# A convolution-attention hybrid on one Trainium2 core: local attention issued in a new order, group norm folded into a product

## Chip, cores and metric

The program runs on one core of one Trainium2 chip. The metric is the device time of one execution in microseconds (us). The core has five instruction queues: TensorE (PE in the profile, with PEld for its weight loads), VectorE (DVE), ScalarE (ACT), GpSimd (POOL) and SyncE (SP), which issues most transfers. Each queue runs in order, and the queues wait for each other by semaphores.

## What is computed

The input is x of 16 images, 56x56 positions, 32 channels, float32. Cut to what matters here:

```python
x = x + local(_gn(x))           # _gn: 32 groups of 1 channel, over H and W, per image
t = x.reshape(16, 3136, 32)
t = t + attention(_ln(t))       # one head over 3136 tokens, plus its input
t = t + experts(_ln(t))         # 16 experts, each pooling its top 8 tokens

def local(x):                   # windows of 7x7, 4 heads of 8 channels, hidden width 128
    h = roll(_ln(x), (3, 3))    # cut into 64 windows of 49 tokens
    q, k, v = split(h @ qkv_w.T + qkv_b)
    a = softmax(q @ k.T / sqrt(8) + bias)
    o = _ln((a @ v) @ out_w.T + out_b)
    return gelu(o @ mlp_w1.T + mlp_b1) @ mlp_w2.T + mlp_b2
```

## The kernel before

The work has four stages. **Setup** loads x in 4 groups of 4 images, brings channels to partitions (4 images x 32 channels = 128) through PE transposes, stores the image with 3 wrapped rows above it in `ximg` (rows of 56), takes the group norm's mean and variance (`gn`) and prepares weights. **Local attention** follows, the stage that the change rewrites. **Global attention** (lines 1607 to 1669) and the **experts** are straight-line code and are not touched.

Local attention runs over 32 chunks (`G * NC`): a chunk is one row of 8 windows of 4 images, that is 392 columns (`CT`) on 128 partitions. A chunk has three parts.

- The part ahead ("pre"): `group_norm` on DVE subtracts the image's mean, scales and wraps 3 columns into `xg`; `center_window` (PE) takes the channel mean away by a product with a constant matrix; ACT squares it, PE averages the squares (`variance`), ACT takes log and exp (`root`), DVE multiplies (`normalize`, k=0); PE forms queries and keys (`project`), ACT and DVE copy them with masks (`queries`, `keys`).
- The main part, four units u of two windows each: `scores` (PE, 8 products), bias added and row maxima (DVE, lines 1047 and 1052), `subtract` (POOL, 544), `exponentials` (ACT, 699), `sums` with a reciprocal (DVE, 1058 and 1061), `probabilities` (POOL, 550), `transposes` (PE, 8 into two banks), `probs_a` (ACT, 703) copies the first bank and `probs_b` (DVE, 1065) the second, `values` (PE) and `values_copy` (DVE, 1072), `weighted_values` (PE, 16 products), `weighted_copy` (ACT, 711).
- The part behind ("post"): `out_projection`, a second norm (k=1), four `hidden` products with four `gelu`, `mlp_out`, `skip_connection` (DVE), `center_sum` and a third norm (k=2), `residual` (POOL), and two stores by SP.

All engines write the work out by hand in a function `chunk(it, ...)` of their own: the post part of chunk it-1, the main part of it and the pre part of it+1 are woven together. The scores, exponentials and probabilities are double buffered by u % 2; the PSUM banks XB, YB and ZB are shared by all the projections and norms. Chunks 0 and 1 (2 and 3 on some engines) and the last two are written out, the rest is a hardware loop (`Fori`) of two chunks an iteration, in which semaphore targets and image rows come from registers. `scores_first` waits for queries and keys and issues a one-column dummy product (line 1425) ahead of unit 0's scores. GELU needs another ACT table set than log and exp do, so a load stands at each change (shown as ACT_TABLE_LOAD, lines 695 and 725).

## Time and profile before

| | us |
|---|---|
| median of 3 runs | 3136.1 (3134.99 to 3137.02) |
| the profiled execution's own time | 3140.94 |
| its span in the profile | 3139.1 |
| setup, to the first `center_window` | 83.2 |
| local attention, first to last `out_projection` (line 1480) | 125.8 to 981.1 |
| experts and stores, from about | 3030 |

A row of the page or of a group of instructions gives the line, the engine, the operation, what it writes and reads with partitions x elements, how often, busy time and mean ns of one, and the idle time before it with what ended it. A row of a timeline gives start, duration and, in brackets, the wait ahead of it. fp32 products appear twice in the counts (x16 for 8 products), and the stated end of a product is modelled: the distance between the starts of two neighbouring groups tells what a group costs PE. PEclk is the clock granted to TensorE as a share of full speed.

### The profile page before, as it was taken

To read this page: it belongs to the slowest core of one execution; us is meant where nothing else is said; L and a number is where in the kernel's file an instruction comes from. 1 tells how busy PE (TensorE), PEld (TensorE's weight loads), DVE (VectorE), ACT (ScalarE), POOL (GpSimd) and SP (SyncE) were. 2 spreads that over 40 slices of the span, in tenths; PEclk is the share of its full clock that TensorE was granted. 3 is DMA by queue.
4 is the path that set the end of the run, shared out by engine and by line. 5 is a ranking of instruction groups with operands and counts; after the bars stand their busy time and mean duration, and the time that the engine had idled before them with its cause. 6 is when DMAs were issued, how large, how long until landed. Compare 5 with 4: busy or idle time off the path is not lost.

```text
span 3139.1 us, 61958 instructions
## 1 busy us (share of the span) xinstructions
PE 2864.7 (91%) x25025; PEld 1320.0 (42%) x25025; DVE 2416.2 (77%) x3155; ACT 2112.6 (67%) x3837; POOL 614.5 (20%) x493
## 2 busy tenths in 40 slices
PE   3788888888886899999999999999999999999987
PEld 3344444444442534344344344344344443443446
DVE  6788888888883787887887877787887877877844
ACT  2477767767764557777777777777777777777762
POOL 0344444444442010110100101101100101101100
PEclk6899999999997989999999999999999999999997
DMA  3000000000002811011011010010110110110003
GB/s 89 1 16 15 15 15 13 13 15 15 15 16 90 286 18 22 1 22 22 1 22 21 2 22 10 13 22 1 22 22 1 22 22 1 22 22 1 1 1 84
DMA packets 93851, 81.05 MB, mean 26 GB/s; under 512 B 62452, under 2 KB 83541, under 8 KB 92629
## 3 DMA queue, kind: packets, MB, share of 16 engines
q1 hardware_dynamic: 92085, 78.26, 9.5%
q8 instruction: 138, 2.26, 0.3%
q14 instruction: 60, 0.49, 0.0%
q10 hardware_dynamic: 1568, 0.04, 0.0%
HBM read 39.57 MB, written 32.11 MB: 23 GB/s over the span
## 4 chain that ended last, share of the span: by engine, by line
PE 68%; issue 11%; ACT 7%; POOL 6%; DVE 5%; DMA 2%; ACTq 1%; POOLq 0%; SPq 0%; DVEq 0%
PE ps L1635 19%; PE ps L1607 18%; PE ps L1659 17%; POOL arena L544 4%; PE ps L1669 3%; PE ps L1619 2%; POOL arena L550 2%; PE ps L1487 1%; ACT arena L699 1%; ACT L725 1%; ACT arena L817 1%; PE ps L1714 1%; DMA arena<-in_x 1%; POOL arena L560 1%; DVE arena L1052 1%
## 5 line engine op out<-in xcount | busy, mean ns | idle before, releaser
L1211 DVE TENSOR_REDUCE arena<-ps 128x2 f32<-128x896 f32 (+1 forms) x1408 | 1455.8, 1078 | 366.9 <-PE ps L1607 366.7
L837 ACT ACTIVATE arena<-ps 128x512 f32<-128x512 f32 (+1 forms) x2464 | 1270.7, 602 | 354.0 <-PE ps L1635 339.7
L1635 PE MATMUL ps<-arena 97*128 97x512 f16 (+1 forms) x2800 | 819.1, 357 | 9.4 <-ACT arena L837 1.2
L1607 PE MATMUL ps<-arena 96*128 96x448 f16 x2800 | 773.1, 358 | 10.8 <-DVE arena L1201 8.2
L1659 PE MATMUL ps<-arena 128*32 128x512 f32 (+2 forms) x7328 | 666.6, 456 | 0.7 <-DVE arena L1233 0.7
L1635 PEld LDWEIGHTS ps<-arena 97*128 97x128 f16 (+1 forms) x2800 | 252.0, 99 | 438.3 <-ACT arena L837 169.8
L1659 PEld LDWEIGHTS ps<-arena 128*32 128x32 f32 x7328 | 235.8, 109 | 408.7 <-ACT arena L837 193.1
L609 POOL TENSOR_TENSOR tok<-arena,tok 128x128 f32<-128x128 f32 (+1 forms) x112 | 47.4, 423 | 1556.4 <-DVE arena L1233 1556.4
L1607 PEld LDWEIGHTS ps<-arena 96*128 96x128 f16 x2800 | 225.2, 99 | 298.5 <-DVE arena L1211 114.4
L550 POOL TENSOR_TENSOR arena<-arena 113x784 f32<-113x784 f32 x128 | 192.4, 1503 | 431.2 <-DVE arena L1061 431.2
L544 POOL TENSOR_TENSOR arena<-arena 113x784 f32<-113x784 f32 x128 | 192.2, 1502 | 129.3 <-DVE arena L1052 129.3
L1058 DVE TENSOR_REDUCE arena<-arena 113x16 f32<-113x784 f32 x128 | 123.6, 965 | 59.9 <-ACT arena L699 59.9
L699 ACT ACTIVATE arena<-arena 113x784 f32<-113x784 f32 x128 | 109.4, 855 | 64.8 <-POOL arena L544 64.5
L1487 PE MATMUL ps<-arena,w1f 128*128 128x392 f32 x256 | 123.1, 565 | 26.0 <-ACT arena L725 23.9
L1458 PE MATMUL ps<-cst,arena 113*128 113x113 f32 x1024 | 127.2, 268 | 10.6 <-POOL arena L550 6.9
L824 ACT ACTIVATE arena<-ps 128x512 f32<-128x512 f32 x96 | 57.3, 597 | 107.9 <-PE ps L1659 107.9
L1052 DVE TENSOR_REDUCE arena<-arena 113x16 f32<-113x784 f32 x128 | 124.2, 970 | 4.5
L1458 PEld LDWEIGHTS ps<-cst,arena 113*128 113x128 f32 x1024 | 104.1, 142 | 41.3 <-POOL arena L550 25.1
L1047 DVE TENSOR_TENSOR arena<-ps,relb 113x784 f32<-113x784 f32 x128 | 116.9, 913 | 2.4 <-PE ps L1432 2.0
L817 ACT ACTIVATE arena<-ps 1x512 f16<-1x512 f32 (+1 forms) x112 | 60.0, 536 | 86.2 <-PE ps L1619 86.0
L1432 PE MATMUL ps<-arena 64*49 64x196 f32 x2048 | 117.1, 344 | 0.1
L1065 DVE COPY arena<-ps 128x452 f32<-128x452 f32 x128 | 79.5, 621 | 45.8 <-PE ps L1458 45.8
(181 smaller groups left out, 2787.6 us busy)
## 6 DMA issues: line engine op xcount, KB each, us to landing
arena<-qk_scratch SPq DMA_DIRECT2D x96, 196.0 KB, 4.0
qk_scratch<-arena SPq DMA_DIRECT2D x16, 448.0 KB, 4.8
arena<-ximg SPq DMA_DIRECT2D x16, 400.0 KB, 6.6
arena<-in_x SPq DMA_DIRECT2D x4, 1568.0 KB, 8.4
xa_scratch<-arena SPq DMA_DIRECT2D x32, 196.0 KB, 1.9
res_scratch<-arena SPq DMA_DIRECT2D x32, 196.0 KB, 2.1
arena<-xa_scratch SPq DMA_DIRECT2D x4, 1568.0 KB, 9.2
arena<-res_scratch SPq DMA_DIRECT2D x4, 1568.0 KB, 13.0
```

Source lines behind the costliest of these rows:

```text
L544: pool.tensor_tensor(s3, s3, mx[0:113, i, :].rearrange("p (m o) -> p m o", o=1) .broadcast_to([113, GB * NH, L]), ALU.subtract).then_inc(c ...
L550: pool.tensor_tensor(pr[0:113, i, :].rearrange("p (m k) -> p m k", k=64)[:, :, 0:L], ex[0:113, i, :].rearrange("p (m k) -> p m k", k=L), m ...
L699: act.activation(ex[0:113, u % 2, :], sc[0:113, u % 2, :], ACT.Exp).then_inc(conv["exp"], 1)
L837: act.activation(pk[0:rows, x % DEPTH, QC * m:QC * m + n], ps[0:rows, w % SB, 0:n], ACT.Exp, scale=float(C) ** -0.5).then_inc(att["exp"], 1)
L1052: dve.tensor_reduce(mx[0:113, i, :], sc[0:113, i, :].rearrange("p (m k) -> p m k", k=L), AX_X, ALU.max)\
L1058: dve.tensor_reduce(mx[0:113, 2 + i, :], ex[0:113, i, :].rearrange("p (m k) -> p m k", k=L), AX_X, ALU.add)\
L1211: dve.tensor_reduce(mxp[0:rows, p, 2 * u:2 * u + k], ps[0:rows, at_:at_ + k, 0:KN], AX_X, ALU.max)\
L1458: last = pe.transpose(ps[:, PT_ + k, 128 * n:128 * n + 113], pr[0:113, i, 128 * m:128 * m + 128], ident(113))
L1487: pe.matmul(ps[:, (XB, XB, XB, YB)[j], 0:CT], w1f[:, j, :], xn2[:, :], start=True, stop=True)\
L1607: last = pe.matmul(ps[0:rows, MB + 2 * (j % 2) + n % 2, 0:KN], q2[p][0:96, T * t:T * t + rows], k2[p][0:96, KN * m:KN * m + KN], start=Tru ...
L1635: last = pe.matmul(ps[0:rows, bank, at_ % QC:at_ % QC + chunk_cols(c)], k2[p][0:97, T * t:T * t + rows], q2[p][0:97, QC * c:QC * c + chunk ...
L1659: last = pe.matmul(ps[C * g:C * (g + 1), AVB, w * h:w * h + w], vf[p][:, t, :], pk[:, x % DEPTH, at_ + w * h:at_ + w * h + w], start=(t < ...
```

## The change

- Every engine's part of local attention is one Python loop over k, without `Fori`: all 32 chunks are straight-line code with constant semaphore targets. A step k works on four chunks: the last norms and the MLP of k, the units of k+1 and k+2, and the centring product of k+3. Waits are written only where the order needs them; the dummy product is gone.
- `group_norm` and `xg` are gone. The group norm's scale is multiplied into the centring matrix, one per image group (`cg`), and its mean into a bias of the product's result (`gnc`), which `square` and `normalize` (k=0) add. `center_window` reads the image itself. `ximg` therefore has rows of 59 (3 wrapped columns) and the product reads it in the order window, row, column, 7 elements at a stretch, where it read 392 in a row before; `normalize` (k=0), which did the reordering, now reads and writes plainly.
- In setup, the statistics are taken from PSUM (7 of 448 elements for 8 of 392), the copy into `ximg` writes rows of 59, and two copies fill the wrapped columns.
- Of the four copies of the second transposed bank in a chunk, those of units 1 and 3 go to ACT (`probs_b`, semaphore `pcopy_c`).

```diff
-        ximg = sb("ximg", [128, G * HALO, W])
+        ximg = sb("ximg", [128, G * HALO, WIDE])
         xf = ximg[:, :, :].rearrange("p r c -> p (r c)")[:, 0:B * NT * C].rearrange(
             "p (t b c) -> p t b c", b=B, t=NT)
...
+                if k == 0:
+                    act.activation(sq[:, :], ps[:, YB, 0:CT], ACT.Square, bias=gnc[:, n // NC:n // NC + 1])\
...
+            def probs_b(u):
+                act.activation(pt[:, u % 2, 4 * 113:8 * 113].rearrange("p (n q) -> p n q", q=113),
+                               ps[:, PT_ + 1, :].rearrange("p (n q) -> p n q", q=128)[:, :, 0:113], ACT.Copy)\
+                   .then_inc(conv["pcopy_c"], 1)
...
+            for k in range(-2, CHUNKS):
+                if on(k):
+                    act.wait_ge(ln[1]["var"], k + 1)
+                    log_of(1)
+                if on(k + 2):
+                    act.wait_ge(ln[0]["center"], k + 3)
+                    square(k + 2, 0)
+                if on(k + 1):
+                    probs_a(0)
+                if on(k):
+                    act.wait_ge(ln[1]["std"], k + 1)
+                    rstd(1)
+                if on(k + 2):
+                    act.wait_ge(ln[0]["var"], k + 3)
+                    log_of(0)
+                    act.wait_ge(ln[0]["std"], k + 3)
+                    rstd(0)
+                if on(k + 1):
+                    act.wait_ge(conv["ptrans"], 8 * k + 12)
+                    probs_a(1)
+                if on(k):
+                    act.wait_ge(conv["hid"], 4 * k + 1)
+                    gelu(0)
+                if on(k + 1):
+                    probs_b(1)
+                    act.wait_ge(conv["av"], 4 * k + 5)
+                    weighted_copy(0)
+                if on(k + 2):
+                    act.wait_ge(conv["qk"], 2 * k + 5)
+                    queries(k + 2)
+                if on(k):
+                    act.wait_ge(conv["hid"], 4 * k + 2)
+                    gelu(1)
+                if on(k + 1):
+                    act.wait_ge(conv["sub"], 4 * k + 8)
+                    exponentials(3)
+                    act.wait_ge(conv["ptrans"], 8 * k + 14)
+                    probs_a(2)
+                    act.wait_ge(conv["av"], 4 * k + 6)
+                    weighted_copy(1)
+                if on(k):
+                    act.wait_ge(conv["hid"], 4 * k + 3)
+                    gelu(2)
+                    act.wait_ge(conv["hid"], 4 * k + 4)
+                    gelu(3)
+                if on(k + 1):
+                    act.wait_ge(conv["av"], 4 * k + 7)
+                    weighted_copy(2)
+                log_and_exp()
+                if on(k + 1):
+                    act.wait_ge(conv["ptrans"], 8 * k + 16)
+                    probs_a(3)
+                if on(k + 2):
+                    act.wait_ge(conv["sub"], 4 * k + 9)
+                    exponentials(0)
+                if on(k + 1):
+                    probs_b(3)
+                if on(k):
+                    act.wait_ge(ln[2]["center"], k + 1)
+                    square(k, 2)
+                if on(k + 1):
+                    act.wait_ge(conv["av"], 4 * k + 8)
+                    weighted_copy(3)
+                if on(k):
+                    act.wait_ge(ln[2]["var"], k + 1)
+                    log_of(2)
+                    act.wait_ge(ln[2]["std"], k + 1)
+                    rstd(2)
+                if on(k + 1):
+                    act.wait_ge(ln[1]["center"], k + 2)
+                    square(k + 1, 1)
+                if on(k + 2):
+                    act.wait_ge(conv["sub"], 4 * k + 10)
+                    exponentials(1)
+                    act.wait_ge(conv["sub"], 4 * k + 11)
+                    exponentials(2)
...
-                img = ximg[:, g * HALO:(g + 1) * HALO, :].rearrange("p r c -> p (r c)")
+                img = image(g, 0, HALO)
                 for n in range(NK):
                     dve.wait_ge(s_xt, NK * g + n + 1)
-                    dve.tensor_copy(img[:, SHIFT * W:].rearrange("p (q j) -> p j q", j=SP)[:, 4 * n:4 * n + 4, :],
-                                    ps[:, n, 0:KN].rearrange("p (j q) -> p j q", j=4)).then_inc(s_xe, 1)
+                    dve.bn_stats(bns[:, n, :], ps[:, n, 0:KN])
+                    dve.tensor_copy(img[:, SHIFT:, SHIFT:].rearrange("p r (h j) -> p j r h", j=SP)[:, 4 * n:4 * n + 4],
+                                    ps[:, n, 0:KN].rearrange("p (j r h) -> p j r h", j=4, h=2)).then_inc(s_xe, 1)
                 dve.wait_ge(s_xe, NK * (g + 1))
-                dve.tensor_copy(img[:, 0:SHIFT * W], img[:, H * W:HALO * W])
-                for c in range(NC):
-                    last = dve.bn_stats(bns[:, c, :], img[:, SHIFT * W + CT * c:SHIFT * W + CT * (c + 1)])
-                step(last)
-                step(dve.bn_aggr(gn[:, g, 0:2], bns[:, :, :].rearrange("p c s -> p (c s)")))
+                dve.tensor_copy(img[:, 0:SHIFT, SHIFT:], img[:, H:HALO, SHIFT:])
+                dve.tensor_copy(img[:, 0:SHIFT, 0:SHIFT], img[:, H:HALO, W:WIDE])
+                step(dve.tensor_copy(img[:, SHIFT:, 0:SHIFT], img[:, SHIFT:, W:WIDE]))
+                step(dve.bn_aggr(gn[:, g, 0:2], bns[:, 0:NK, :].rearrange("p c s -> p (c s)")))
...
             step(dve.reciprocal(gn[:, :, 3], gn[:, :, 2]))
+            for g in range(G):
+                last = dve.tensor_scalar(cg[:, g, :], cv("center"), gn[:, g, 3:4], None, ALU.mult)
+            step(last)
...
+            dve.tensor_scalar(gnc[:, :], ps[:, 6, 0:G], -1.0, None, ALU.mult)
...
                 if k == 0:
-                    def rows(v):
-                        return v.rearrange("p (r w c) -> p r w c", r=WS, c=WS)
-                    last = dve.tensor_tensor(dst.rearrange("p (w r c) -> p r w c", r=WS, c=WS), rows(src),
-                                             rows(rs[:, k, :]), ALU.mult)
+                    dve.scalar_tensor_tensor(xn[:, n % 2, :], ps[:, YB, 0:CT], gnc[:, n // NC:n // NC + 1], rs[:, 0, :], ALU.add,
+                                             ALU.mult).then_inc(ln[0]["norm"], 1)
...
+                if on(k):
+                    dve.wait_ge(conv["y"], 2 * k + 2)
+                    if on(k - 1):
+                        dve.wait_ge(conv["rt"], k)
+                    skip_connection(k)
...
+            for g in range(G):
+                pe.matmul(ps[:, 6, g:g + 1], cg[:, g, :], gn[:, g, 0:1], start=True, stop=True)
             pe.matmul(ps[:, 4, 3:4], wp[:, 256:384], bv[:, BV:BV + 1], start=True, stop=False)
...
             def center_window(n):
-                pe.wait_ge(conv["xg"], n + 1)
-                pe.matmul(ps[:, YB, 0:CT], cv("center"), xg[:, :], start=True, stop=True).then_inc(ln[0]["center"], 1)
+                pe.matmul(ps[:, YB, 0:CT], cg[:, n // NC, :],
+                          image(n // NC, n % NC * WS, WS)[:, :, 0:W].rearrange("p r (w c) -> p w r c", c=WS),
+                          start=True, stop=True).then_inc(ln[0]["center"], 1)
...
+            for k in range(-3, CHUNKS):
+                if on(k + 2):
+                    pe.wait_ge(ln[0]["norm"], k + 3)
+                    project_queries(k + 2)
+                    project_keys(k + 2)
+                if on(k):
+                    pe.wait_ge(conv["gelu"], 4 * k + 1)
+                    hidden(1)
+                if on(k + 1):
+                    pe.wait_ge(conv["pcopy_c"], 2 * k + 3)
+                    pe.wait_ge(conv["prob"], 4 * k + 7)
+                    transposes(2)
+                    pe.wait_ge(conv["oc"], 4 * k + 5)
+                    values(k + 1, 2)
+                if on(k + 2):
+                    pe.wait_ge(conv["kz"], k + 3)
+                    pe.wait_ge(conv["qz"], k + 3)
+                    scores(0)
+                if on(k + 1):
+                    pe.wait_ge(conv["vcopy"], 4 * k + 7)
+                    weighted_values(1)
+                if on(k):
+                    pe.wait_ge(conv["gelu"], 4 * k + 2)
+                    hidden(2)
+                    hidden(3)
+                if on(k + 2):
+                    pe.wait_ge(conv["bias"], 4 * k + 9)
+                    scores(1)
+                if on(k + 1):
+                    pe.wait_ge(conv["pcopy_b"], 2 * k + 4)
+                    pe.wait_ge(conv["oc"], 4 * k + 6)
+                    weighted_values(2)
+                if on(k):
+                    mlp_out((0, 1))
+                    pe.wait_ge(conv["gelu"], 4 * k + 4)
+                    mlp_out((2, 3))
+                if on(k + 1):
+                    pe.wait_ge(conv["prob"], 4 * k + 8)
+                    transposes(3)
+                    pe.wait_ge(conv["oc"], 4 * k + 7)
+                    values(k + 1, 3)
+                if on(k):
+                    pe.wait_ge(conv["t1"], k + 1)
+                    center_sum(k)
+                if on(k + 2):
+                    pe.wait_ge(conv["bias"], 4 * k + 10)
+                    scores(2)
+                if on(k + 1):
+                    pe.wait_ge(conv["pcopy_c"], 2 * k + 4)
+                    pe.wait_ge(conv["vcopy"], 4 * k + 8)
+                    weighted_values(3)
+                if on(k):
+                    pe.wait_ge(ln[2]["square"], k + 1)
+                    variance(2)
+                if on(k + 1):
+                    pe.wait_ge(conv["oc"], 4 * k + 8)
+                    out_projection(k + 1)
+                if on(k + 2):
+                    values(k + 2, 0)
+                    pe.wait_ge(conv["prob"], 4 * k + 9)
+                    transposes(0)
+                if on(k + 1):
+                    pe.wait_ge(ln[1]["square"], k + 2)
+                    variance(1)
+                if on(k + 3):
+                    if on(k):
+                        pe.wait_ge(ln[2]["norm"], k + 1)
+                    center_window(k + 3)
+                if on(k + 2):
+                    pe.wait_ge(conv["vcopy"], 4 * k + 9)
+                    values(k + 2, 1)
+                    scores(3)
+                if on(k + 3):
+                    pe.wait_ge(ln[0]["square"], k + 4)
+                    variance(0)
+                if on(k + 2):
+                    pe.wait_ge(conv["pcopy_a"], 4 * k + 9)
+                    pe.wait_ge(conv["pcopy_b"], 2 * k + 5)
+                    pe.wait_ge(conv["prob"], 4 * k + 10)
+                    transposes(1)
+                if on(k + 1):
+                    pe.wait_ge(ln[1]["norm"], k + 2)
+                    hidden(0)
+                if on(k + 2):
+                    pe.wait_ge(conv["vcopy"], 4 * k + 10)
+                    weighted_values(0)
+            pe.wait_ge(ln[2]["norm"], CHUNKS)
```

The two places that follow show how instructions stand in the steady state. PE around the projections, before. Line 1507 and 1508 are queries' and keys' projections, 1487 is `hidden`, 1446 `values`, 1458 `transposes`, 1473 `weighted_values`, 1425 the dummy, 1432 `scores`, 1493 `mlp_out`.

```order
L1507 MATMUL ps<-arena,wp 128x392
L1508 MATMUL ps<-arena,wp 128x392
L1487 MATMUL ps<-arena,w1f 128x392
L1446 MATMUL ps<-wp,arena 49x128 x4
L1458 MATMUL ps<-cst,arena 128x113 x8
L1487 MATMUL ps<-arena,w1f 128x392
L1473 MATMUL ps<-arena 32x49 x16
L1425 MATMUL ps<-cst 1x1
L1432 MATMUL ps<-arena 49x196 x8
L1487 MATMUL ps<-arena,w1f 128x392
L1493 MATMUL ps<-arena,w2t 32x392 x4
```

The same place of the change: 1498 and 1502 project, 1477 is `hidden`, 1454 `transposes`, 1445 `values`, 1435 `scores`, 1466 `weighted_values`, 1483 `mlp_out`.

```order
L1498 MATMUL ps<-arena,wp 128x392
L1502 MATMUL ps<-arena,wp 128x392
L1477 MATMUL ps<-arena,w1f 128x392
L1454 MATMUL ps<-cst,arena 128x113 x8
L1445 MATMUL ps<-wp,arena 49x128 x4
L1435 MATMUL ps<-arena 49x196 x8
L1466 MATMUL ps<-arena 32x49 x16
L1477 MATMUL ps<-arena,w1f 128x392 x2
L1435 MATMUL ps<-arena 49x196 x8
L1466 MATMUL ps<-arena 32x49 x16
L1483 MATMUL ps<-arena,w2t 32x392 x4
```

Unit 0's scores moved from behind five other groups to behind three, the second and third scores stand among the MLP's products, and `mlp_out` follows two score groups instead of directly following the last `hidden`.

ACT from the first GELU to the end of the MLP, before (725 is `gelu`, 711 `weighted_copy`, 703 `probs_a`, 719 `queries`, 699 `exponentials`):

```order
L725 ACT_TABLE_LOAD
L725 ACTIVATE arena<-ps,bv 128x392
L711 ACTIVATE arena<-ps 128x2x7x7
L725 ACTIVATE arena<-ps,bv 128x392
L703 ACTIVATE arena<-ps 128x452
L719 ACTIVATE arena<-ps,bv 128x392 x2
L695 ACT_TABLE_LOAD
L699 ACTIVATE arena<-arena 113x784
L711 ACTIVATE arena<-ps 128x2x7x7
L725 ACT_TABLE_LOAD
L725 ACTIVATE arena<-ps,bv 128x392 x2
L695 ACT_TABLE_LOAD
```

Of the change (732 `gelu`, 712 `probs_b`, 719 `weighted_copy`, 726 `queries`, 702 `exponentials`, 706 `probs_a`, 698 the explicit table load):

```order
L732 ACT_TABLE_LOAD
L732 ACTIVATE arena<-ps,bv 128x392
L712 ACTIVATE arena<-ps 128x452
L719 ACTIVATE arena<-ps 128x2x7x7
L726 ACTIVATE arena<-ps,bv 128x392 x2
L732 ACTIVATE arena<-ps,bv 128x392
L702 ACT_TABLE_LOAD
L702 ACTIVATE arena<-arena 113x784
L706 ACTIVATE arena<-ps 128x452
L719 ACTIVATE arena<-ps 128x2x7x7
L732 ACT_TABLE_LOAD
L732 ACTIVATE arena<-ps,bv 128x392 x2
```

The number of table loads in a chunk is four in both; a `probs_b` came in, and `queries` stands ahead of the second GELU.

## Rows read from the trace of the kernel before

**Rows 1.** Windows: PE, PEld, DVE, ACT, POOL busy (instructions), PEclk, DMA share, GB/s

```profile
235.00:313.00 78.00, 65.62 (x815) 34.84 (x810) 65.39 (x99) 55.63 (x88) 38.35 (x27) 1.00 0.04 15
392.00:470.00 78.00, 67.44 (x810) 35.42 (x808) 63.38 (x95) 53.27 (x87) 37.42 (x27) 0.96 0.04 15
1260.00:3020.00 1760.00, 1752.04 (x12931) 713.44 (x12931) 1397.06 (x1652) 1276.83 (x2472) 179.55 (x178) 1.00 0.07 13
```

**Rows 2.** Line 1480, `out_projection`, all 32 of them

```profile
L1480 PE MATMUL ps<-arena,wp x64: 492/545/598, 125.8 to 981.4; 128*128 128x392 f32 x64
```

**Rows 3.** PE's timeline in one chunk of the loop, 407 to 436 us

```profile
409.67 0.56 PE L1473 MATMUL ps<-arena 113*32 113x49 f32 x32
410.16 0.93 PE L1507 MATMUL ps<-arena,wp 128*128 128x392 f32 x2
...
412.48 0.90 PE L1487 MATMUL ps<-arena,w1f 128*128 128x392 f32 x2 [0.74 <-ACT arena L725]
413.31 0.65 PE L1446 MATMUL ps<-wp,arena 128*49 128x128 f32 x8
...
418.06 0.19 PE L1425 MATMUL ps<-cst 128*1 128x1 f32 x2 [1.72 <-DVE arena L1097]
418.18 0.88 PE L1432 MATMUL ps<-arena 64*49 64x196 f32 x16
418.99 1.06 PE L1487 MATMUL ps<-arena,w1f 128*128 128x392 f32 x2
419.98 2.49 PE L1493 MATMUL ps<-arena,w2t 128*32 128x392 f32 x8
...
429.27 0.99 PE L1458 MATMUL ps<-cst,arena 113*128 113x113 f32 x8
430.10 0.84 PE L1415 MATMUL ps<-arena,cst 128*128 128x392 f32 x2
```

**Rows 4.** ACT's timeline, 407 to 436 us: the GELU ahead of the product at 412.48

```profile
411.75 0.59 ACT L725 ACTIVATE arena<-ps,bv 128x392 f32<-128x392 f32 x1
```

**Rows 5.** Groups by line, 100 to 920 us, DVE, ACT and line 1493

```profile
L699 ACT ACTIVATE arena<-arena 113x784 f32<-113x784 f32 x120 | 102.6, 855 | 61.2 <-POOL arena L544 60.9
...
L725 ACT ACT_TABLE_LOAD x58 | 74.4, 1283 | 1.0
...
L1065 DVE COPY arena<-ps 128x452 f32<-128x452 f32 x119 | 73.9, 621 | 40.3 <-PE ps L1458 40.3
L1097 DVE TENSOR_SCALAR arena<-ps,cst,bv 128x392 f32<-128x392 f32 x120 | 73.7, 676 | 0.0
...
L703 ACT ACTIVATE arena<-ps 128x452 f32<-128x452 f32 x119 | 65.0, 546 | 47.6 <-PE ps L1458 47.6
L1493 PE MATMUL ps<-arena,w2t 128*32 128x392 f32 x232 | 57.6, 566 | 0.0
...
L1040 DVE TENSOR_SCALAR arena<-ximg,gn 128x371 f32 (+1 forms) x30 | 37.6, 1253 | 0.0
```

**Rows 6.** Timelines of DVE and ACT in setup: the last statistics, the square root

```profile
60.39 0.37 DVE L964 BATCH_NORM_AGGREGATE gn<-bns 128x2 f32<-128x48 f32 x1
65.83 0.30 ACT L675 ACTIVATE gn<-gn,cst 128x4 f32<-128x4 f32 x1
```

**Rows 7.** DVE and PE in setup, 0 to 90 us

```profile
L1403 PE MATMUL ps<-pv,wbd 128*128 128x1 f32 x6 | 1.4, 356 | 4.7 <-DVE wp L1006 4.7
...
L1005 DVE TENSOR_SCALAR wp<-wbd,pv 128x128 f32<-128x128 f32 x1 | 0.3, 280 | 0.0
```

**Rows 8.** PE's timeline in the experts: line 1804, straight-line code of short products

```profile
3078.21 1.69 PE L1804 MATMUL ps<-arena,ximg 128*32 128x16 f32 x128 [2.18 <-issue]
3081.96 0.54 PE L1804 MATMUL ps<-arena,ximg 128*32 128x16 f32 x15 [2.06 <-issue]
```

**Rows 9.** DMA queues in a stretch of the loop, 235 to 500 us

```profile
DMA packets 2880, 4.02 MB, mean 15 GB/s; under 512 B 320, under 2 KB 2880, under 8 KB 2880
...
q1 hardware_dynamic: 2880, 4.02, 4.2%
```

More of the change, by code:

```diff
@@ L266, in image, with on @@
         def image(g, row, rows):
-            return ximg[:, bass.ds(g * HALO + row, rows), :]
+            return ximg[:, g * HALO + row:g * HALO + row + rows, :]
+        def on(n):
+            return 0 <= n < CHUNKS
         def tile_rows(t):
@@ L1584, in _, with project_queries @@
-            n = G * NC - 1
-            out_projection(n)
-            pe.wait_ge(ln[2]["std"], n)
-            variance(n, 1)
-            for j in range(GB):
-                if j == 3:
-                    pe.wait_ge(ln[2]["norm"], n)
-                hidden(n, j)
-            mlp_out(n)
-            center_sum(n)
-            variance(n, 2)
-            pe.wait_ge(ln[2]["norm"], G * NC)
+            def project_queries(n):
+                pe.matmul(ps[:, YB, 0:CT], wp[:, 0:128], xn[:, n % 2, :], start=True, stop=True).then_inc(conv["qk"], 1)
```

453 lines of the change are left out of this document (136 added, 317 removed).

## The prediction

> **What bounds the kernel now.** I read first the windows of the busy times. In local attention PE is busy 65.6 of 78 us, DVE 65.4, ACT 55.6, POOL 38.4 [rows 1]: no engine is full, while in global attention PE is busy 1752 of 1760 us. That stage can be shortened only by less PE work, and the change doesn't touch it; local attention has room on every engine. Next is the length of a chunk: the 32 `out_projection`s run from 125.8 to 981.4 us, 31 intervals in 855.6 us, so **27.6 us a chunk** [rows 2]. Last is PE's timeline in one chunk, for what PE does and where it stands [rows 3]. It waited 1.72 us for the last of DVE's four key copies ahead of unit 0's scores, 0.74 us for a GELU that holds the bank of the next `hidden`, and five times 0.2 to 0.4 us (the bracketed waits of the same view), 3.9 us in all. After the long wait the same product also costs more: `hidden` 0.99 us to the next start at 418.99 for 0.83 at 412.48, and the MLP's output products 2.49 us for a mean of 1.99 (57.6 us over 29 chunks) [rows 3, 5]. In that window the granted clock is 0.96 where it is 1.00 in others and in all of global attention [rows 1]. So PE is the engine nearest to full, and what bounds a chunk is the circle of waits between PE, ACT and DVE, with some clock lost behind them.
>
> **PE's own work in a chunk.** By distances between starts [rows 3]: 12 products of 392 columns (three variances, two centrings, the output projection, four `hidden`, two projections) at 0.83 = 10.0; four `scores` at 0.81 = 3.2; four `transposes` at 0.83 = 3.3; four `weighted_values` at 0.49 = 2.0; four `values` at 0.58 (0.65 stated, less the 0.07 by which neighbours overlap) = 2.3; the MLP's 2.0 [rows 5]. Sum **22.8 us**. No order can make a chunk shorter, at these prices.
>
> **The other engines after the change.** DVE had 65.4/78 x 27.6 = 23.1 us of work. It loses the group norm (1.25 us [rows 5] and a short second instruction, 0.27 as I read it from the same view) and two copies of 0.62, and gains 0.06 where a product becomes one with a bias: 20.4. ACT had 19.7 and gains two copies of 0.55 and a bias: 20.9; the four table loads of 1.28 stay, as the order shows. POOL keeps 13.6. All lie under 22.8, so PE stays the bound if the waits are covered.
>
> **The timetable.** I laid out one step k: each queue in its new order, each instruction at the duration of its row, 0.1 us for a handoff (the GELU of 411.75 ended at 412.34, the product behind it began at 412.48 [rows 3, 4]), and let the step repeat. Three paths close within half a microsecond of each other.
> - PE alone: 22.8.
> - Keys: with 0 at the queries' projection, the keys' projection is done at 1.7, DVE's four copies of 0.62 each (0.68 stated [rows 5]) end at 4.2, so unit 0's scores start at 4.3. PE gets there at 1.6 + 0.83 + 0.83 + 0.58 = 3.85. It waits 0.45: **23.2**. Before, that wait was 1.72.
> - ACT's run: from `variance(0)` of chunk k+3 through Ln, Exp, `probs_a`, load, GELU, `probs_b`, `weighted_copy`, queries, GELU, load, exponential, `probs_a`, `weighted_copy`, load, two GELUs: 0.6 + 0.5 + 0.5 + 1.3 + 0.6 + 0.5 + 0.25 + 1.2 + 0.6 + 1.3 + 0.86 + 0.5 + 0.25 + 1.3 + 1.1 = 11.4 [rows 4, 5]. Then PE from the MLP's second half through 13 groups back to `variance(0)`: 1.0 + 9.7 + 0.83, and two handoffs: 11.7. Together 23.1.
>
> The moved waits. `skip_connection` on DVE now stands in front of maxima, `values_copy` and `sums`; DVE comes to it at 9.2 and the MLP ends at 10.7, so it stands 1.5 us there and delays all of these; yet `center_sum` is reached at 12.0 and the sums are in time for the transposes at 16.3. The centring product for k+3 waits for the third norm of k (ready at 17.7, reached at 18.0). SP's stores of k-1 are issued at the end of `residual`, 17 us ahead of the next write of `xa`. `probs_b` on ACT is due at 2.1 for transposes reached at 2.4, behind the first GELU, which stands behind a table load: here cover is thinnest, 0.3 us.
>
> From 23.2 I go to **23.4**: the clock lost 0.7 us a chunk behind a wait of 1.72 (0.16 at `hidden`, 0.5 at the MLP), and a wait of 0.45 stays. Price of the stage: 31 x (27.6 - 23.4) = -130 us. Filling (first centring to first output projection) and draining have the same chains as before; I cost them at nothing, with 5 us either way.
>
> **The strided read.** The trace has no product that reads 7 elements at a stretch. Below, it costs nothing: the plain product takes 0.83 us for 392 columns, 2.1 ns a column. Above, I take it to double, +0.83 a chunk. I choose nothing, since a column at that rate is slower than anything else the engine does here: 32 products of 49 columns pass in 0.49 us [rows 3], 0.3 ns a column.
> [...]
>
> **Setup.** Added behind the group norm's statistics, on the path: four scalings of 128x128 at 0.28, about 1.0; four products on PE (eight instructions at 0.24, the six of line 1403 took 1.4), 1.9; a small copy 0.15 [rows 7]; off: the first chunk's group norm, 0.8. Together +2.2, between +1 and +4. The dearer copies into rows of 59 end at about 61 us, where the last statistics ended at 60.8, and the square root behind them began at 65.8, held by ACT's own queue of transfers [rows 6]: 4 us of cover; without it they would cost up to 1 us.
>
> **Sum.** -130 + 2.2 = -128 against the profiled execution's 3140.9: 3013. The median of the runs is 4.8 us lower, so on its scale **3008 us**.
>
> **The rivals.**
> - *The read is dear.* +0.83 on an engine that is full: 24.2 a chunk, 31 x 3.4 = 105 less 2: 3033. For: the only product of its kind. Against: a row of products at a rate far from the engine's fastest. [...] Chance 0.13.
> - *The waits move but stay.* ACT's run has 0.3 us of cover; each late table load moves the MLP, then the third norm, then the next run. If half of today's 3.9 us returns, a chunk is 23.2 + 2.0 = 25.2, saving 74 less 2: 3064. For: three paths of nearly equal length, on queues in order. Against: ACT and DVE have 10% of slack. Chance 0.2.
> - *Slower: instructions come late.* In the loop all DMA packets are of the data queue [rows 9]: its code is fetched once. After, each chunk brings 289 products on PE, 578 instructions. In the experts' straight-line code PE ran 128 products (256 instructions with the weight loads) and then stood 2.1 us with nothing to wait for but issue, a block every 3.75 us [rows 8]. If each block of 256 cost that in the stage too, 2.26 x 2.1 = 4.7 us come onto 23.2: 27.9 a chunk, +9 and +2 for setup: 3147. It decides from 1.95 us a block. Against: that code asked for 256 instructions in 1.7 us, a chunk asks for 578 in 23, and 256 in 3.75 us is 68 a microsecond against 25. Chance 0.05.
>
> **How the numbers follow.** Forecast (22.8 to 24.0 a chunk): 0.57. With the two rivals that gain less, and 0.03 for shorter or longer chunks than any of these, faster is 0.93. The rest to one: 0.02 for within 0.2% (6 us, about what a measurement of this kernel can tell from no change), 0.05 for slower. The low end is a full PE, 31 x 4.8 = 149: 2989, and 3 for the fill: 2986. The high end takes in the dear read and half of the second rival: 3055.
>
> **What would show it.** Right: intervals of the output projection of 23.2 to 23.6; PE over 95% busy in the stage with the clock at 1.00; the wait ahead of unit 0's scores about 0.45 and on DVE's keys; DVE waiting for the MLP at `skip_connection`; no issue wait on PE; the centring product at 0.83 to the next start. Wrong: that product near 1.6; waits of PE on ACT over 1 us a chunk; waits for issue every 256 instructions; clock under 0.97 without waits.

## The result, and the profile after

The changed kernel takes 2967.3 us (median of 4 runs, 2965.9 to 2968.4), the kernel before 3136.6 beside it (3135.0 to 3138.3). The ratio is 0.9461 [0.9448, 0.9473]: 169 us less. The forecast was 3008 with a range of 2986 to 3055, so the direction was right, and the time lies 19 us under the low end of the range.

From part 1 of the two pages (busy us, share of the span, instructions), before and after, and the queue that carries code, after:

```profile
PE 2864.7 (91%) x25025; PEld 1320.0 (42%) x25025; DVE 2416.2 (77%) x3155; ACT 2112.6 (67%) x3837; POOL 614.5 (20%) x493
...
PE 2810.3 (95%) x24969; PEld 1316.9 (44%) x24969; DVE 2332.2 (79%) x3036; ACT 2118.4 (71%) x3903; POOL 613.3 (21%) x493
...
q8 instruction: 197, 3.23, 0.5%
```

The same two windows as in [rows 1], now of the kernel after:

```profile
235.00:313.00 78.00, 76.99 (x1010) 44.02 (x1008) 70.69 (x107) 68.38 (x117) 47.13 (x33) 1.00 0.06 22
392.00:470.00 78.00, 76.68 (x976) 44.02 (x975) 70.80 (x108) 69.56 (x119) 46.30 (x33) 1.00 0.06 22
```

PE went from 65.6 and 67.4 busy of 78 us to 77.0 and 76.7, and the granted clock of the second window from 0.96 to 1.00. `out_projection`, line 1473 now, over its 32 chunks (duration min/median/max in ns, first and last start):

```profile
L1473 PE MATMUL ps<-arena,wp x64: 492/492/597, 127.3 to 809.1; 128*128 128x392 f32 x64
```

Counted from first start to last group (808.8), that is 681.5 us for 31 intervals, **21.98 us a chunk**, where [rows 2] gave 27.6. The span fell by 174.3 us: the stage gives 173.7 to 174, setup and fill take 1.5 (127.3 for 125.8), the work behind the stage gives 2.0. The profiled execution was 4.4 us above the median before and 0.7 below it after, which is why the medians differ by only 169.

Where the time on PE came from is in the list of its waits in the stage (us in total, times, longest). Before, 125 to 981 us:

```profile
PE ps L1425 <- DVE arena L1097: 52.0, 30, 1.9
PE ps L1487 <- ACT arena L725: 22.4, 30, 2.3
```

After, 127 to 809 us:

```profile
PE ps L1435 <- DVE arena L1107: 10.0, 30, 0.3
PE ps L1454 <- POOL arena L554: 1.2, 1, 1.2
```

All such waits add up to 128 us before and 14 after. The page's PE busy time fell from 2864.7 to 2810.3, 54 us more, with nearly the same products (25,025 and 24,969): what is left for that is the clock, and waits that lay inside groups and counted as busy. 114 + 54 is 168 of the span's 174.

One chunk on PE after (timeline: start, duration, wait ahead of it in brackets):

```profile
399.79 0.93 PE L1498 MATMUL ps<-arena,wp 128*128 128x392 f32 x2
...
403.94 0.88 PE L1435 MATMUL ps<-arena 64*49 64x196 f32 x16 [0.34 <-DVE arena L1107]
...
407.93 1.57 PE L1483 MATMUL ps<-arena,w2t 128*32 128x392 f32 x8
409.43 0.99 PE L1454 MATMUL ps<-cst,arena 113*128 113x113 f32 x8
...
416.67 0.86 PE L1488 MATMUL ps<-ximg,arena 128*128 128x392 f32 x2
417.46 0.65 PE L1445 MATMUL ps<-wp,arena 128*49 128x128 f32 x8
...
418.85 0.93 PE L1428 MATMUL ps<-arena,cst 128*128 128x392 f32 x2
...
421.82 0.93 PE L1498 MATMUL ps<-arena,wp 128*128 128x392 f32 x2
```

ACT over the same stretch and the next one:

```profile
407.53 1.06 ACT L732 ACTIVATE arena<-ps,bv 128x392 f32<-128x392 f32 x2
...
419.81 0.59 ACT L690 ACTIVATE arena<-ps,cst 128x392 f32<-128x392 f32 x1 [0.66 <-PE ps L1428]
...
421.41 1.28 ACT L732 ACT_TABLE_LOAD   x1
...
423.19 0.54 ACT L712 ACTIVATE arena<-ps 128x452 f32<-128x452 f32 x1
423.62 0.27 ACT L719 ACTIVATE arena<-ps 128x98 f32<-128x98 f32 x1
...
425.51 1.28 ACT L702 ACT_TABLE_LOAD   x1
...
428.26 1.28 ACT L732 ACT_TABLE_LOAD   x1
429.56 1.07 ACT L732 ACTIVATE arena<-ps,bv 128x392 f32<-128x392 f32 x2
```

Read together they show a closed loop. The last two GELUs of a chunk end at 407.53 + 1.06 = 408.59; PE, which had the first half of the MLP's output products out, finishes the second half and goes on with no wait in brackets to `variance` at 418.85; ACT stands 0.66 us for it and starts its Ln at 419.81; from there it runs with no wait through three table loads to the end of the next two GELUs, 429.56 + 1.07 = 430.63. That is 11.22 on PE (handoffs included) and 10.82 on ACT, **22.04 us**, the length of a chunk (22.03 between the starts at 399.79 and 421.82). Any two parts of a schedule that repeats add up to its period; what makes these two a loop that can bind is that neither holds a wait. The MLP's group shows no wait in brackets, because the wait lies inside it; the experiments show it.

On DVE the skip connection, which waits for the MLP:

```profile
409.55 0.63 DVE L1115 SCALAR_TENSOR_TENSOR arena<-ps,pv,ximg 128x392 f32<-128x392 f32 x1 [0.79 <-PE ps L1483]
```

### The profile page after: what moved, and what is told of

Same layout as the page of the kernel before. It is cut to its first block, busy times and chain, and to the rows that moved or that the text cites. A ratio compares the mean times of both kernels' runs of the same rounds, so it can differ in the third digit from the quotient of the medians.

```text
span 2964.8 us, 60107 instructions
## 1 busy us (share of the span) xinstructions
PE 2810.3 (95%) x24969; PEld 1316.9 (44%) x24969; DVE 2332.2 (79%) x3036; ACT 2118.4 (71%) x3903; POOL 613.3 (21%) x493
## 3 DMA queue, kind: packets, MB, share of 16 engines
q8 instruction: 197, 3.23, 0.5%
## 4 chain that ended last, share of the span: by engine, by line
PE 85%; DVE 7%; ACT 4%; DMA 2%; issue 1%; ACTq 1%; POOL 0%; POOLq 0%; SPq 0%; DVEq 0%
PE ps L1630 20%; PE ps L1602 20%; PE ps L1654 18%; PE ps L1435 4%; PE ps L1664 3%; PE ps L1428 3%; DVE arena L1107 3%; PE ps L1454 2%; PE ps L1614 2%; PE ps L1445 2%; PE ps L1477 2%; PE ps L1466 2%; PE ps L1483 1%; ACT arena L841 1%; PE ps L1709 1%
## 5 line engine op out<-in xcount | busy, mean ns | idle before, releaser
L549 POOL TENSOR_TENSOR arena<-arena 113x784 f32<-113x784 f32 x128 | 192.3, 1502 | 202.8 <-DVE arena L1066 202.8
L1477 PE MATMUL ps<-arena,w1f 128*128 128x392 f32 x256 | 112.0, 540 | 4.4 <-ACT arena L732 2.4
L1664 PEld LDWEIGHTS ps<-wvo,arena 128*128 128x128 f32 (+1 forms) x800 | 103.7, 189 | 20.6 <-issue 6.4
```

What stands on the lines that cost most here:

```text
L549: pool.tensor_tensor(s3, s3, mx[0:113, u % 2, :].rearrange("p (m o) -> p m o", o=1) .broadcast_to([113, GB * NH, L]), ALU.subtract).then_i ...
L1477: pe.matmul(ps[:, (XB, XB, XB, YB)[j], 0:CT], w1f[:, j, :], xn2[:, :], start=True, stop=True)\
L1664: last = pe.matmul(ps[0:rows, AVB, (C + 1) * i:(C + 1) * (i + 1)], ua[:, T * i:T * i + rows], wvo[:, :], start=True, stop=True)
```

## The experiments

"The loop of ACT and PE" below is the one just described. Ratios are to the kernel before, run beside each on the same chip; chunk lengths are the distance from first to last `out_projection` over 31. The kernel before took 3137 us beside the result and 3138 to 3141 beside the experiments, so a difference of up to 4 us between two experiments may be no difference. All edits but the first change the kernel after. Of each edit the main lines are shown; waits that have to follow it are left out.

**1. Order or loops?** The kernel before, its four engines' loops written out, order untouched:

```diff
-            with pe.Fori(0, G * NC // 2 - 2) as i:
+            for i in range(G * NC // 2 - 2):
                 chunk(i * 2 + 2, 0)
```

> The kernel before with its local-attention loops on PE, DVE, ACT and POOL written out (32 chunks of straight-line code), order and waits as they were. Theory that the new order brings nearly all of the gain: a chunk stays near 27.2 us, since only the group norm's first instruction on DVE gets cheaper (1.25 us in the loop); 3125 us, between 3115 and 3137. Rival, that a good part comes from leaving the loop (registers for semaphore targets, branches): 3095 us or less. Rival, that straight-line code costs by late instructions: above 3140.

3131.2 us, 0.9974 [0.9964, 0.9984]. Its `out_projection`:

```profile
L1480 PE MATMUL ps<-arena,wp x64: 492/545/597, 125.9 to 971.8; 128*128 128x392 f32 x64
```

27.3 us a chunk. Straight-line code costs nothing here and is worth 8 us (5 to 11); the other 161 are from what the chunk does and in which order.

**2. The copies on ScalarE.** Both second-bank copies (`probs_b` of units 1 and 3) back on DVE:

```diff
                 if on(k + 1):
-                    probs_b(1)
                     act.wait_ge(conv["av"], 4 * k + 5)
...
                 if on(k + 1):
+                    dve.wait_ge(conv["ptrans"], 8 * k + 12)
+                    probs_b(1)
                     dve.wait_ge(conv["score"], 4 * k + 8)
...
                     values_copy(3)
+                    probs_b(3)
```

> The changed kernel with all four copies of the second bank on DVE again. Theory that DVE's key copies end the one wait of PE that is left (0.34 us a chunk) and that a copy ahead of them delays them by its 0.55 us: 31 x 0.5 = +16, 2983 us, wait ahead of unit 0's scores 0.85 us. Rival, that the copies are hidden on either engine: 2967, within 3 us.

2969.3 us, 0.9452 [0.9432, 0.9472]: no difference from the kernel after (0.9461). PE's timeline, and ACT's with the last two GELUs:

```profile
404.38 0.88 PE L1435 MATMUL ps<-arena 64*49 64x196 f32 x16 [0.84 <-DVE arena L1104]
...
408.38 0.98 PE L1483 MATMUL ps<-arena,w2t 128*32 128x392 f32 x8
409.29 1.00 PE L1454 MATMUL ps<-cst,arena 113*128 113x113 f32 x8
```

```profile
405.82 0.26 ACT L719 ACTIVATE arena<-ps 128x98 f32<-128x98 f32 x1 [0.24 <-PE ps L1466]
...
407.39 1.07 ACT L732 ACTIVATE arena<-ps,bv 128x392 f32<-128x392 f32 x2
```

The wait for the keys grew by 0.5 as expected, but the time did not follow: the MLP's group now takes 0.91 us to the next start where it took 1.50. So PE had 0.6 us of waiting in that group, and the eight instructions cost 0.91 at most. At most, since even here the last GELU ends inside the group, at 407.39 + 1.07 = 408.46, and the next group starts 0.83 behind that end, as in the kernel after (409.43 - 408.59 = 0.84). This run took my full PE away as an explanation.

The edit makes two changes that cancel. Unit 1's copy is gone from ACT's run, where it took 0.43 (423.19 to 423.62 above); with the loop alone as the bound that would have been worth 13 us. But ACT now stands 0.24 us inside its run for `weighted_values(1)` (line 1466), which come behind the scores that waited 0.84 for DVE's keys. So a path through DVE's keys lies less than half a microsecond under the loop, and takes over when ACT's run gets shorter.

**3. A read with a step.** The centring product reads the same columns in another order, so that in each column of seven an element lies 59 floats from the one before. Its output has the positions in that order, so this kernel leaves out the layer's right order and serves for the time alone:

```diff
-  image(n // NC, n % NC * WS, WS)[:, :, 0:W].rearrange("p r (w c) -> p w r c", c=WS),
+  image(n // NC, n % NC * WS, WS)[:, :, 0:W].rearrange("p r (w c) -> p w c r", c=WS),
```

> The changed kernel with the centring product of the image reading down the columns (each next element 59 elements or 236 bytes on) instead of 7 neighbours at a stretch; the windows then hold their positions in another order, so the output is another. It moves no other work. Theory that a product at this rate doesn't feel the pattern of its read: 2967, group to next start 0.79 us as now. Rival, the rule that each read of another 16-byte line costs: the product above 1.2 us, 2980 us or more.

2988.7 us, 0.9512 [0.9491, 0.9533], 21 us more than the kernel after. The product and its successor on PE, then the same two in the kernel of experiment 7, where the product reads whole rows:

```profile
403.69 1.52 PE L1488 MATMUL ps<-ximg,arena 128*128 128x392 f32 x2
405.14 0.65 PE L1445 MATMUL ps<-wp,arena 128*49 128x128 f32 x8
```

```profile
400.44 0.82 PE L1499 MATMUL ps<-arena,cst 128*128 128x392 f32 x2
401.19 0.65 PE L1455 MATMUL ps<-wp,arena 128*49 128x128 f32 x8
```

1.45 us to the next start, where runs of seven elements take 0.79 (416.67 to 417.46 above) and whole rows 0.75. My expectation of no cost was wrong for this step and right for the change's own read. The chunk grew by 0.65 (22.63): all of the dearer product, which stands in PE's part of the loop.

**4. The MLP directly behind `hidden`.**

```diff
                     hidden(3)
+                    mlp_out((0, 1))
+                    pe.wait_ge(conv["gelu"], 4 * k + 3)
+                    mlp_out((2,))
+                    pe.wait_ge(conv["gelu"], 4 * k + 4)
+                    mlp_out((3,))
...
-                if on(k):
-                    mlp_out((0, 1))
-                    pe.wait_ge(conv["gelu"], 4 * k + 4)
-                    mlp_out((2, 3))
```

> The changed kernel with the MLP's four output products directly behind the hidden products, each of the last two with a wait for its GELU, as the kernel before had them. Theory that the 1.99 us that the prediction took for them was 1.50 of work and the rest waits inside the group: PE stands there for the last two GELUs (they end near 8.6 us after the queries' projection, PE is there at 7.0), some 1.2 us a chunk less what the moved groups take up elsewhere: 2985 to 3007 us, the group's busy time 2.0 us or more. Rival, that the group costs the same wherever it stands and slack takes up the wait: 2967, within 5 us.

3018.6 us, 0.9613 [0.9593, 0.9632], 51 us more than the kernel after, a little over the top of what I expected; 23.57 us a chunk.

```profile
402.43 0.85 PE L1483 MATMUL ps<-arena,w2t 128*32 128x392 f32 x4
403.85 1.32 PE L1483 MATMUL ps<-arena,w2t 128*32 128x392 f32 x4 [0.56 <-ACT arena L732]
405.10 0.88 PE L1435 MATMUL ps<-arena 64*49 64x196 f32 x16
...
409.89 0.56 PE L1466 MATMUL ps<-arena 113*32 113x49 f32 x32 [0.26 <-ACT arena L712]
```

The MLP takes 2.67 us to the next start instead of 1.50. `scores(1)` and `weighted_values(2)`, which stand between the last `hidden` and the MLP in the kernel after (one score group there, not two), were done there while ACT worked on the GELUs; now they come behind them, inside PE's part of the loop. They take 0.81 and 0.49, and a new wait of 0.26 for one of ACT's copies comes on top: 1.56 of the 1.59 by which the chunk grew.

**5. More waits.** Four more waits a chunk on PE, for conditions that mostly hold already: one ahead of each of the MLP's four products, where one stood ahead of the third, and one ahead of `hidden(3)`:

```diff
-                    mlp_out((0, 1))
-                    pe.wait_ge(conv["gelu"], 4 * k + 4)
-                    mlp_out((2, 3))
+                    for j in range(GB):
+                        pe.wait_ge(conv["gelu"], 4 * k + j + 1)
+                        mlp_out((j,))
```

> The changed kernel with four more waits on PE a chunk (one ahead of each MLP output product, one ahead of the fourth hidden product), on semaphores that were reached before in most cases. Theory that a wait already satisfied costs nothing: 2967, within 3 us; the group of MLP products 1.50 us to the next start. Rival, that a wait keeps the weight load from running ahead and costs about 0.1 us each: +13, 2980 us, the group near 1.9.

2967.9 us, 0.9453 [0.9440, 0.9466], 22.0 us a chunk. The waits cost nothing that shows; they stand where PE has up to 0.9 us to spare, so this doesn't show that a wait that is met is free. ACT's last two GELUs and the group behind the MLP:

```profile
406.68 1.07 ACT L732 ACTIVATE arena<-ps,bv 128x392 f32<-128x392 f32 x2
```

```profile
408.57 0.99 PE L1454 MATMUL ps<-cst,arena 113*128 113x113 f32 x8
```

Only one product stands behind the last GELU now, where two did, and the next group still starts 0.82 us after that GELU's end (0.84 in the kernel after). So a product fewer behind the GELU doesn't shorten PE's part of the loop.

**6. One product more.** Is PE full?

```diff
                     pe.wait_ge(ln[0]["norm"], k + 3)
+                    pe.matmul(ps[:, YB, 0:CT], wp[:, 0:128], xn[:, k % 2, :], start=True, stop=True)
                     project_queries(k + 2)
```

> The changed kernel with one more product of 392 columns a chunk (the queries' projection once more, of other data, then overwritten). Theory that PE is the bound: +0.76 x 32 = +24, 2991 us. Rival, that a circle of waits with slack on PE is the bound: less than +12.

2971.1 us, 0.9464 [0.9448, 0.9479]: 4 us at most for 32 products of 0.77, which a full PE would have paid with 25; the chunk grew by 0.08. The extra product stands in the stretch where ACT is in its run, and the slack in the MLP's group takes it (PE, then ACT):

```profile
402.20 0.93 PE L1507 MATMUL ps<-arena,wp 128*128 128x392 f32 x2
402.97 0.82 PE L1498 MATMUL ps<-arena,wp 128*128 128x392 f32 x2
...
411.00 0.98 PE L1483 MATMUL ps<-arena,w2t 128*32 128x392 f32 x8
411.91 0.99 PE L1454 MATMUL ps<-cst,arena 113*128 113x113 f32 x8
```

```profile
410.01 1.07 ACT L732 ACTIVATE arena<-ps,bv 128x392 f32<-128x392 f32 x2
```

0.91 again, and again 0.83 behind the last GELU's end at 411.08: the loop still binds. A PE that is 98% busy in a window is not what bounds it.

**7. The group norm outside the weights.** DVE normalizes the chunk into a buffer as before, ahead of unit 0's sums, and the centring product takes the plain weights (the bias `gnc` is zero):

```diff
-                pe.matmul(ps[:, YB, 0:CT], cg[:, n // NC, :],
-                          image(n // NC, n % NC * WS, WS)[:, :, 0:W].rearrange("p r (w c) -> p w r c", c=WS),
-                          start=True, stop=True).then_inc(ln[0]["center"], 1)
+                pe.wait_ge(conv["xg"], n + 1)
+                pe.matmul(ps[:, YB, 0:CT], cv("center"), xg[:, :], start=True, stop=True).then_inc(ln[0]["center"], 1)
```

> The changed kernel with the group norm on DVE again (one instruction a chunk, mean and scale from a constant address, written ahead of unit 0's sums), and the plain centring matrix. Theory that DVE has slack and the fold brings little by itself: DVE some 0.6 us more a chunk, hidden but for 0.0 to 0.2 us: 2965 to 2975 us. Rival, that the fold is a main part of the gain: +0.6 us a chunk or more, 2986 us or more.

2983.0 us, 0.9504 [0.9488, 0.9519], 16 us more than the kernel after, 22.48 us a chunk. I had allowed for less. DVE and POOL in one chunk:

```profile
417.45 1.23 DVE L1122 TENSOR_SCALAR arena<-ximg,gn 128x392 f32<-128x392 f32 x1
```

```profile
416.93 1.50 POOL L550 TENSOR_TENSOR arena<-arena 113x784 f32<-113x784 f32 x1 [1.05 <-DVE arena L1067]
```

With 1.23 us more on DVE the sums of probabilities come late, POOL divides late, and PE's transposes wait for it (14.4 us over the stage in the group of line 1464, 1.2 in the kernel after). Another place in DVE's order might cost less; none was tried.

**8. `hidden(2)` ahead of `scores(0)`**, so that PE has work while DVE finishes the keys:

```diff
+                if on(k):
+                    pe.wait_ge(conv["gelu"], 4 * k + 2)
+                    hidden(2)
                 if on(k + 2):
...
                 if on(k):
-                    pe.wait_ge(conv["gelu"], 4 * k + 2)
-                    hidden(2)
                     hidden(3)
```

> The changed kernel with the third hidden product ahead of unit 0's scores, where PE waits 0.34 us for DVE's key copies. Theory that only PE's time counts: the wait shrinks to 0.0 to 0.15 us, -0.2 x 32 = -6, 2961 us. Rival, that bias and maxima of unit 0, 0.4 us later, delay DVE's run and give it back: 2967 or more.

2969.8 us, 0.9457 [0.9443, 0.9470]: no gain. The wait for the keys is gone, and the MLP's group takes 1.72 us instead of 1.50: PE waits there for the same GELU. The two waits are one slack in two places.

**9 and 10. The loop itself.** A spare copy of 392 columns on ACT, once in its run between Ln and the last GELU, once outside it:

```diff
                     probs_a(1)
+                    act.activation(spare[:, :], cst[:, 0:CT], ACT.Copy)
```

> The changed kernel with one more copy of 392 columns on ACT a chunk (of constants, into a spare buffer), placed inside ACT's run between the variance of k+3 and the last GELU. Circle theory (ACT's run of 10.8 us and PE's stretch of 11.1 us from the MLP's second half back to that variance bound a chunk): +0.45 to 0.55 a chunk, +14 to +17, 2981 to 2984 us. Rival, that PE's work bounds a chunk: 2967, within 4 us.

```diff
                     weighted_copy(3)
+                    act.activation(spare[:, :], cst[:, 0:CT], ACT.Copy)
```

> The same spare copy on ACT, placed behind the last weighted copy, where ACT waits 0.57 us for a variance, outside its run. Circle theory: hidden, 2967 within 4 us, although ACT's busy time is the same as in the kernel with the copy inside. Rival, that ACT's total (88% busy) or its load at large is what counts: as in that kernel, +14 or more.

Inside: 2981.4 us, 0.9503 [0.9489, 0.9518], 22.40 us a chunk, +0.42. Outside: 2968.4 us, 0.9458 [0.9443, 0.9472], 21.99. The same instruction costs 0.42 us a chunk in the one place and nothing in the other. PE with the copy inside:

```profile
405.56 0.93 PE L1479 MATMUL ps<-arena,w1f 128*128 128x392 f32 x2 [0.36 <-ACT arena L733]
...
412.88 0.85 PE L1485 MATMUL ps<-arena,w2t 128*32 128x392 f32 x4 [0.24 <-ACT arena L733]
```

Here the wait for the GELU that was inside the MLP's group comes out as one in brackets.

**11 and 12. Trying to shorten the loop.** First, `variance(0)` of chunk k+3 ahead of `scores(3)`, with experiment 8's edit:

```diff
                     values(k + 2, 1)
-                    scores(3)
                 if on(k + 3):
...
                 if on(k + 2):
+                    scores(3)
                     pe.wait_ge(conv["pcopy_a"], 4 * k + 9)
```

> The changed kernel with two moves on PE: the first norm's variance ahead of unit 3's scores, and the third hidden product ahead of unit 0's scores. Circle theory: PE's stretch in the circle is 0.4 us shorter (the square ends at 0.4 us before PE gets to the variance now), a chunk 21.6, -12, 2955 us (2952 to 2960). Rival, that PE is the bound: the new wait of 0.4 us ahead of the variance adds to it, 2967 or more.

Then the same with `probs_b` of unit 1 on DVE (experiment 2's edit, unit 1 alone), which takes 0.4 us out of ACT's run:

```diff
                 if on(k + 1):
-                    probs_b(1)
                     act.wait_ge(conv["av"], 4 * k + 5)
```

> As the kernel with the two moves on PE, and with unit 1's copy of the second bank on DVE, which takes 0.45 us out of ACT's run; unit 3's stays on ACT. Circle theory: the circle is 21.1 us, then PE with 21.1 of work and a wait of 0.4 is next, 21.5 a chunk: -15, 2952 us (2945 to 2957). Rival, that DVE (then over 93% busy) and its copies ahead of the keys give it back: 2960 or more.

2974.5 us, 0.9478 [0.9465, 0.9491], and 2970.1 us, 0.9465 [0.9452, 0.9478]: 7 and 3 us more than the kernel after (the 3 not clear of the noise), where I expected 12 and 15 less. PE and ACT in the first of them:

```profile
420.46 0.93 PE L1428 MATMUL ps<-arena,cst 128*128 128x392 f32 x2 [0.25 <-ACT arena L681]
...
422.13 0.99 PE L1454 MATMUL ps<-cst,arena 113*128 113x113 f32 x8
```

```profile
422.04 0.53 ACT L694 ACTIVATE arena<-arena 128x392 f32<-128x392 f32 x1
423.16 0.55 ACT L706 ACTIVATE arena<-ps 128x452 f32<-128x452 f32 x1 [0.59 <-PE ps L1454]
```

Ln and Exp do come first now, but the next instruction of ACT's run is `probs_a(1)`, which needs the transposes, and these I had put behind `scores(3)`: ACT waits 0.59 us for them. The loop has two entries from PE, the variance and the transposes, so moving the variance alone can't shorten it. The variance now waits for ACT as well (0.25, line 681). In the second, ACT's run holds a further wait, the one of experiment 2:

```profile
406.29 0.26 ACT L719 ACTIVATE arena<-ps 128x98 f32<-128x98 f32 x1 [0.18 <-PE ps L1467]
```

No version that I ran is faster than the kernel after.

## Why the prediction was right in direction and wrong in size

- **The bound before** ("the circle of waits between PE, ACT and DVE, with some clock lost behind them"): right. The waits went from 128 to 14 us and the clock to 1.00. In the chunk of [rows 3] the clock was at half for 3 us, which cost 1.5 us at most; part of that time PE would have waited for the GELUs in any case, so my 0.7 isn't refuted. Over 150 to 780 us it was 0.98, which makes about 0.5 a chunk. Windows of the kernel before, under the MLP of that chunk:

```profile
419.00:420.00 1.00, 1.00 (x8) 0.30 (x4) 0.96 (x3) 0.99 (x2) 0.26 (x1) 0.82 0.00 0
420.00:423.00 3.00, 3.00 (x15) 1.13 (x16) 1.48 (x3) 2.18 (x3) 2.67 (x2) 0.50 0.00 0
```

- **"PE's own work 22.8 ... No order can make a chunk shorter, at these prices"**: this is the step that failed. The chunk is 21.98. Summed from the distances in the timeline after, PE's work is 21.1: the MLP costs 0.91 at most, not 1.99, and the twelve products of 392 columns 9.24 together, 0.77 each, not 0.83. The first is the large error. 1.99 was the mean busy time of a group in [rows 5], and this group waits for GELUs inside itself and partly ran at half clock; in [rows 3] it is 2.49, while its two last GELUs ended only at 420.90 (ACT's row below), 0.9 us after it began. I took a wait and a slow clock for a price, and then used it as a floor, which also set the low end of the range at 2986.

```profile
419.84 1.06 ACT L725 ACTIVATE arena<-ps,bv 128x392 f32<-128x392 f32 x2
```

- **The keys' path, 23.2 with a wait of 0.45**: the wait is there on DVE's line 1107, at 0.34, but it isn't the bound; experiments 2 and 8 made it 0.84 and 0 with no change in time. It lies close under the bound, though: in experiment 2 it took over, since ACT's run had got shorter.
- **"ACT's run ... 11.4 ... 11.7. Together 23.1"**: the right mechanism, mis-sized. Measured 10.82 + 11.22 = 22.04. I had three paths within half a microsecond and took the wrong one for the last. Experiment 9 against 10 shows the loop to be the bound (+0.42 for a copy inside, +0.01 outside), and 3 (+0.65), 4 (+1.6) and 6 (+0.08) agree with it; 2 and 12 agree only together with the keys' path. ACT's part was too long since I summed durations: 423.19 + 0.54 is 423.73, but the next instruction starts at 423.62. The Trainium skill has this in "ScalarE: Activation LUTs", section "What ACT_TABLE_LOAD costs": back-to-back activations overlap by about 93 ns; the trace agrees with 0.11. PE's part was too long by the two prices above. Adding the 0.2 for a clock that stays low was wrong too: it is 1.00. Of the 1.42 us by which a chunk is shorter than forecast, 0.2 is that clock, 0.1 the choice of the keys' path, 0.6 ACT's part and 0.5 PE's.
- **In microseconds**: 23.4 - 21.98 = 1.42 a chunk, 31 times, 44 us; the fill 0.7 and the drain 2.0 come on top, and 5.5 are taken back because the two profiled executions stand differently to their medians. Together 41, against 3008 - 2967 = 41.
- **Setup, +2.2**: the first centring product starts 1.8 us later, the first `out_projection` 1.5. Right.
- **The strided read**: right to take next to no price: 0.79 us to the next start, for 0.75 with whole rows in the same place. The argument for it was weaker than it looked: the group counted as x32 in [rows 3] is 16 products, each counted twice, so a column passes there in 0.6 ns, not 0.3. Experiment 3 shows that the rival was real for another pattern. The Trainium skill, in "Advanced Engine Details and Errata", section "Memory Cachelines", says of SBUF that an access to a different 16-byte line each time pays a penalty and that two hits on a line are needed to absorb the latency. The traces agree: where each element is 236 bytes from the last the product costs 0.66 us more on 392 columns, and in runs of 28 bytes, which hit most lines twice or more, hardly anything.
- **Waits that move but stay**: it did not happen as priced: 0.34 in brackets and 0.59 hidden in the MLP are what is left of 3.9. DVE stands 0.79 us at `skip_connection`, not 1.5, since the MLP is done sooner.
- **Instructions late**: no wait for issue on PE in the stage; the instruction queue q8 moved 3.23 MB for 2.26, 59 packets more, and experiment 1 shows straight-line code, of the old order, at no cost.
- **The parts.** The fold into the centring weights is worth 16 us where the instruction stood in experiment 7, the copies on ACT 2 or nothing (experiment 2), straight-line code 8 (experiment 1, on the kernel before). The rest, some 140, is the order together with the waits and the dummy product that went; I did not measure it alone, and parts taken out of two different kernels need not add up.

What stays open: why 392-column products take 0.67 to 0.85 us depending on their neighbours, and whether the loop gets shorter if variance and transposes are both moved ahead, or if the exponential between the GELUs is moved so that two of the table loads (1.28 each) go. Neither was tried, and the keys' path is likely to limit either gain.

## What to carry to other kernels

Price an operation by the distance between starts, at full clock, in a place where nothing waited; a busy time hides waits inside a group, and a floor built from such prices is too high. When several engines are 90 to 98% busy, lay the waitless stretches of two of them end to end: if they close into a loop of one period, that loop is likely the bound. What is added inside it costs its full length; outside it, only what exceeds the slack there. What is taken out of it gains only down to the next path, which here lay less than half a microsecond below. The cheapest test is one spare instruction, once inside and once outside.

## What the runs showed of the hardware that I had not expected

- An fp32 product of 392 columns takes 1.45 us when its moving operand steps 59 floats from element to element, 0.79 in runs of seven, 0.75 in whole rows.
- After PE had stood 1.72 us for the keys, its clock was granted at 0.82, and then for 3 us at 0.50, the lower level (1.2 GHz), which lay under the MLP; with waits of 0.34 us a chunk, and of 0.84 in experiment 2, it stays at 1.00.
- The four products of the MLP, each into 32 rows of the output from 392 columns, take 0.91 us together at most, hardly more than one product of 392 columns into 128 rows; and behind a GELU one of them or two cost the same 0.83.
- The group norm's instruction on DVE, fp32 from SBUF to SBUF, took 0.50 us once, in setup while POOL was idle, on 371 columns, and 1.23 on 392 in the stage, where POOL's subtraction runs beside it in the rows of experiment 7. That POOL is the cause wasn't tested by itself; the fold took it off DVE in either case.
